# Window attention laid over eight shared PSUM banks, with new orders on all engines

## The reference, cut to what matters

```python
qkv = xw @ qkv_w + qkv_b                       # xw: (B * 16 windows, 64 tokens, 64 channels)
q, k, v = (split(t) for t in jnp.split(qkv, 3, axis=-1))          # 4 heads of 16
scores = jnp.einsum('bhqd,bhkd->bhqk', q, k)
scores = scores / jnp.maximum(qn * kn.transpose(0, 1, 3, 2), 1e-06) / jnp.clip(tau, 0.01)[None, :, None, None]
scores = scores + bias[None]                   # a table over relative positions, from a small MLP
scores = scores.reshape(B, NW, HEADS, TOK, TOK) + _MASK[None, :, None]
attn = jax.nn.softmax(scores.reshape(B * NW, HEADS, TOK, TOK), axis=-1)
out = jnp.einsum('bhqk,bhkd->bhqd', attn, v)   # then heads side by side
om = out @ proj_w + proj_b                     # windows back to image, rolled back
skip = xin + _layer_norm(om, ln1_g, ln1_b)
```

## Time and profile before

| what | us |
|---|---|
| median of 3 runs | 783.17 (781.18 to 783.38) |
| span of the profiled execution, first to last instruction | 778.6 |
| its own time beside the span | not listed; the median is 4.6 above the span |
| TensorE busy | 665.7 (86%) |
| VectorE busy | 516.4 (66%) |
| ScalarE busy | 480.4 (62%) |
| GpSimd busy | 355.1 (46%) |

### The profile page before, as it was taken

How to read it: one execution, slowest core, us unless ns; L and a number is a source line. 1 busy time by engine, 2 the same in 40 slices (tenths; PEclk the granted TensorE clock), 3 DMA queues, 4 the chain that set the end, 5 groups by cost and what they waited for, 6 DMA issues and landing times. The chain is left out here.

```text
span 778.6 us, 21192 instructions
## 1 busy us (share of the span) xinstructions
PE 665.7 (86%) x8584; PEld 371.4 (48%) x8584; DVE 516.4 (66%) x997; ACT 480.4 (62%) x963; POOL 355.1 (46%) x441
## 2 busy tenths in 40 slices
PE   4785789999999999999998579999999988749880
PEld 2562455565565555655555232233333367735350
DVE  4796487877777787877778322577777786372181
ACT  3565266777777777777775548877777656624000
POOL 4696446778777777788776520022221123100000
PEclk9787599999999999999999959999999999969955
DMA  9550000000000000000000020122112220120278
GB/s 216 137 128 11 1 3 2 3 2 3 2 3 3 3 3 3 3 2 3 3 2 3 2 56 1 28 55 56 33 50 55 55 55 2 31 72 2 63 194 269
DMA packets 15719, 31.44 MB, mean 40 GB/s; under 512 B 7488, under 2 KB 9284, under 8 KB 15620
## 3 DMA queue, kind: packets, MB, share of 16 engines
q1 hardware_dynamic: 12592, 29.16, 14.1%
q10 hardware_dynamic: 2760, 0.66, 0.5%
q0 software_dynamic: 272, 0.27, 0.2%
HBM read 20.71 MB, written 9.37 MB: 39 GB/s over the span
## 5 line engine op out<-in xcount | busy, mean ns | idle before, releaser
L794 POOL TENSOR_TENSOR sc<-sc,mx 128x512 f32<-128x512 f32 x128 | 133.7, 1044 | 102.4 <-DVE mx L725 102.4
L722 DVE TENSOR_TENSOR sc<-s_ps,bias_tab 128x512 f32<-128x512 f32 x128 | 87.7, 685 | 52.6 <-PE s_ps L528 52.6
L1424 POOL TENSOR_TENSOR square<-xs 128x1024 f32<-128x1024 f32 x16 | 34.1, 2133 | 165.5 <-DVE xs L1166 165.5
L539 PE MATMUL t_ps<-consts,sc 128*128 128x128 f32 x512 | 84.4, 288 | 16.2 <-ACT pt L656 12.5
L656 ACT ACTIVATE pt<-t_ps 128x512 f32<-128x512 f32 x128 | 75.7, 592 | 31.2 <-PE t_ps L539 30.1
L539 PEld LDWEIGHTS t_ps<-consts,sc 128*128 128x128 f32 x512 | 54.3, 142 | 84.8 <-issue 48.1
L725 DVE TENSOR_REDUCE mx<-sc 128x8 f32<-128x512 f32 x128 | 87.8, 686 | 4.4
L1081 ACT ACTIVATE hs<-h_ps,fb1s 128x512 f32<-128x512 f32 x128 | 78.2, 689 | 19.1 <-PE h_ps L990 19.0
L528 PE MATMUL s_ps<-kx,qu 32*64 32x128 f32 x2048 | 72.3, 278 | 3.5 <-DVE kx L749 2.9
L990 PE MATMUL h_ps<-xs,fw 64*128 64x512 f32 x256 | 68.7, 650 | 1.0 <-ACT hs L1081 1.0
L528 PEld LDWEIGHTS s_ps<-kx,qu 32*64 32x64 f32 x2048 | 56.7, 134 | 15.2 <-issue 13.4
(11 more groups left out here) (207 smaller groups left out, 1295.2 us busy)
## 6 DMA issues: line engine op xcount, KB each, us to landing
raw<-in_x_dram SPq DMA_DIRECT2D x32, 256.0 KB, 5.1
xr<-in_x_dram SPq DMA_DIRECT2D x32, 256.0 KB, 3.9
out_dram<-x SPq DMA_DIRECT2D x32, 256.0 KB, 3.9
rec_scratch<-r SPq DMA_DIRECT2D x4, 224.0 KB, 2.5
w<-in_L_conv_W_dram SPq DMA_DIRECT2D x1, 784.0 KB
w<-in_L_conv_W_dram SPq DMA_DIRECT2D x1, 672.0 KB
xs<-rec_scratch SPq DMA_DIRECT2D x16, 28.0 KB
xs<-rec_scratch ACTq DMA_DIRECT2D x16, 28.0 KB
```

The costliest lines, as they stand in the source:

```text
L539: last = pe.transpose(t_ps[:, m], sc[n % KEPT][:, m].rearrange("c h k -> c (h k)"), ident)
L722: dve.tensor_tensor(sc[n % KEPT][:, :, :, :], s_ps[j][:, :, :, :], bias_tab[:, j, hp], ALU.add)\
L794: pool.tensor_tensor(v, v, mx[n % KEPT][:, :].unsqueeze(2).broadcast_to([128, 8, TOK]), ALU.subtract)\
```

## The change

All eight banks become one tensor, `banks`, and each use names its bank; a bank passes from one use to the next by a semaphore. `score` runs twice a pair instead of four times: both halves `hp` of the head pairs at once, 32 matmuls on four row strips and two column halves, into four banks. Transposes have banks by turns instead of one; the sums are a group of their own (`sums`), apart from `mix`. `spread_rstd` has four matmuls of 32 rows into four banks, without the half-zero weights. Work on two 512-column halves becomes one instruction of 1024 columns on VectorE (bias, maximum, scaling) and ScalarE (copies; the spread of values in 4 instructions instead of 8). GpSimd keeps 512 columns each. `qu`, `kx`, `ob` exist once; score tiles, now double in size, three times. The four lists are new and run for 20 steps, and the special code for the last pair is gone.

```diff
-    def score(pe, p, q):
-            a, hp = q // 2, q % 2
-            pe.wait_ge(s["queries"], 2 * p + a + 1)
-            pe.wait_ge(s["keys_odd"], 2 * p + a + 1)
-            after(pe, s["biased"], 2 * (4 * p + q))
-            for i, m, w in WINDOWS:
-                for j in range(2):
-                    row = rows(2 * j + hp)
-                    last = pe.matmul(s_ps[j][TOK * w:TOK * (w + 1), 2 * i + m], qu[p % 2][a][row, at],
-                                     kx[p % 2][a][row, :, at], start=True, stop=True)
+    SCORE_BANKS = ((6, 2), (4, 6))
+    TURN_BANKS = {(0, 0): (2, 3), (0, 1): (5, 4), (1, 0): (5, 4), (1, 1): (0, 7)}
+    SUM_BANKS, MIX_BANKS = (5, 0), (6, 4)
+    def score(pe, p, a):
+            if a == 0:
+                pe.wait_ge(s["queries"], p + 1)
+                pe.wait_ge(s["keys_odd"], p + 1)
+                if there(p + 1, PAIRS):
+                    pe.wait_ge(s["q_out"], p + 2)
+            else:
+                pe.wait_ge(s["biased_00"], p + 1)
+                after(pe, s["heads_0"], p)
+                after(pe, s["exped_11"], 2 * p)
+                after(pe, s["normed"], 2 * (p - 2) + 2)
+            for i in range(2):
+                for m in range(2):
+                    for w in range(2):
+                        at = slice(TOK * (4 * i + 2 * m + w), TOK * (4 * i + 2 * m + w + 1))
+                        for j in range(2):
+                            for hp in range(2):
+                                row = rows(2 * j + hp)
+                                out_bank = banks[:, SCORE_BANKS[a][hp] + j].rearrange("c (m n) -> c m n", m=4)
+                                last = pe.matmul(out_bank[TOK * w:TOK * (w + 1), 2 * i + m], qu[row, a, at],
+                                                 kx[row, a, :, at], start=True, stop=True)
...
     def spread_rstd(pe, p):
-            for h in range(2):
-                for j, (lo, hi) in enumerate(HALVES):
-                    last = pe.matmul(spread_bank(p, j)[:, 256 * h:256 * (h + 1)], spread_half[lo:hi, h], rv[lo:hi, :],
+            for g in range(4):
+                last = pe.matmul(banks[:, 2 + g, 0:256], spread_image[rows(g)], rv[rows(g), :], start=True, stop=True)
...
+    def add_bias(dve, p, a, hp):
...
+            dve.tensor_tensor(sc[n % KEPT][:, :, :, :, :].rearrange("c j m h k -> c (j m h k)"),
+                              banks[:, first:first + 2].rearrange("c j n -> c (j n)"),
+                              bias_tab[:, hp].rearrange("c j m h k -> c (j m h k)"), ALU.add)\
+               .then_inc(s[f"biased_{a}{hp}"], 1)
+    def row_max(dve, p, a, hp):
...
+            dve.tensor_reduce(mx[n % KEPT][:, :], sc[n % KEPT][:, :, :, :, :].rearrange("c j m h k -> c (j m h) k"),
+                              X, ALU.max).then_inc(s[f"row_max_{a}{hp}"], 1)
...
     def tensor_step(pe, n):
+        project_keys(pe, n)
+        turn(pe, n - 2, 1, 0, 1)
+        score(pe, n - 1, 0)
+        sums(pe, n - 2, 0)
+        variances(pe, n - 3)
+        turn(pe, n - 2, 1, 1, 0)
+        turn(pe, n - 2, 1, 1, 1)
+        mix(pe, n - 2, 0)
+        spread_rstd(pe, n - 3)
+        norms(pe, n)
+        sums(pe, n - 2, 1)
+        score(pe, n - 1, 1)
+        turn(pe, n - 1, 0, 0, 0)
+        turn(pe, n - 1, 0, 0, 1)
+        values(pe, n - 1)
+        mix(pe, n - 2, 1)
+        spread_first(pe, n)
+        turn(pe, n - 1, 0, 1, 0)
+        turn(pe, n - 1, 0, 1, 1)
+        project_heads(pe, n - 2)
+        turn(pe, n - 1, 1, 0, 0)
+        project_queries(pe, n + 1)
     def vector_step(dve, n):
+        scale_keys(dve, n - 1, 1)
+        add_bias(dve, n - 1, 0, 0)
+        add_bias(dve, n - 1, 0, 1)
+        row_max(dve, n - 1, 0, 0)
+        divide(dve, n - 2, 0)
+        normalise(dve, n - 3, 0)
+        normalise(dve, n - 3, 1)
+        row_max(dve, n - 1, 0, 1)
+        add_bias(dve, n - 1, 1, 0)
+        add_bias(dve, n - 1, 1, 1)
+        row_max(dve, n - 1, 1, 0)
+        divide(dve, n - 2, 1)
+        row_max(dve, n - 1, 1, 1)
+        scale_queries(dve, n)
+        scale_keys(dve, n, 0)
     def scalar_step(act, n):
+        copy_queries(act, n)
+        exponent(act, n - 2, 1, 0, 0)
+        copy_keys(act, n)
+        exponent(act, n - 2, 1, 0, 1)
+        sum_log(act, n - 2, 0)
+        var_rstd(act, n - 3)
+        sum_exp(act, n - 2, 0)
+        exponent(act, n - 2, 1, 1, 0)
+        exponent(act, n - 2, 1, 1, 1)
+        norm_recip(act, n)
+        sum_log(act, n - 2, 1)
+        sum_exp(act, n - 2, 1)
+        by_rows(act, n - 3, 0, 0)
+        exponent(act, n - 1, 0, 0, 0)
+        exponent(act, n - 1, 0, 0, 1)
+        by_rows(act, n - 3, 0, 1)
+        by_rows(act, n - 3, 1, 0)
+        spread_values(act, n - 1)
+        by_rows(act, n - 3, 1, 1)
+        exponent(act, n - 1, 0, 1, 0)
+        exponent(act, n - 1, 0, 1, 1)
+        copy_projected(act, n - 2)
     def pool_step(pool, n):
+        square_projected(pool, n - 3, 0)
+        square_projected(pool, n - 3, 1)
+        square(pool, n, q_sb, q_sq, "q_out", "q_sq")
+        square(pool, n, k_sb, k_sq, "k_out", "k_sq")
+        shift(pool, n - 1, 0, 0)
+        skip(pool, n - 3, 0)
+        skip(pool, n - 3, 1)
+        shift(pool, n - 1, 0, 1)
+        shift(pool, n - 1, 1, 0)
+        shift(pool, n - 1, 1, 1)
```

More of the change, by code:

```diff
@@ L418, in build @@
                 "k_ps", "q_ps", "k_out", "q_out", "k_sq", "q_sq", "norm_ps", "norm_ln", "rnorm", "first_spread",
[L419 to L424, removed]
+                "keys_even", "keys_odd", "queries", "v_ps", "v_out", "heads_0", "heads_1", "proj_ps", "proj_out", "csq",
@@ L432, in build @@
[L432 to L445, removed]
@@ L512, in spread_first @@
+                    for a in range(2):
+                        last = pe.matmul(banks[:, 6 + a], spread_keys[rows(a)], rn[rows(a), :], start=True, stop=True)
                     last.then_inc(s["first_spread"], 1)
-                    for a in range(2):
-                        last = pe.matmul(b_ps[a][:, :], spread_all[rows(2 + a)], rn[rows(2 + a), :], start=True, stop=True)
-                    last.then_inc(s["first_spread"], 1)
-            def score(pe, p, q):
+            def score(pe, p, a):
@@ new lines, in sums @@
+            def sums(pe, p, a):
+                if there(p, PAIRS):
+                    pe.wait_ge(s[f"exped_{a}0"], 2 * p + 2)
+                    pe.wait_ge(s[f"exped_{a}1"], 2 * p + 2)
+                    if a == 0:
+                        pe.wait_ge(s["exped_10"], 2 * p + 1)
+                    for j in range(2):
+                        for hp in range(2):
+                            last = pe.matmul(banks[rows(2 * j + hp), SUM_BANKS[a]], ones, pt[a][2 * hp + j][:, :, :],
+                                             start=True, stop=True)
+                    last.then_inc(s[f"sum_ps_{a}"], 1)
@@ L542, in mix @@
             def mix(pe, p, a):
                 if there(p, PAIRS):
[L545 to L552, removed]
+                    pe.wait_ge(s["v_out"], p + 1)
@@ L581, in variances @@
                     pe.wait_ge(s["csq"], 2 * p + 2)
[L582 to L585, removed]
+                    if there(p + 3, PAIRS):
+                        pe.wait_ge(s["k_out"], p + 4)
                     for g in range(4):
                         half = slice(256 * (g % 2), 256 * (g % 2 + 1))
-                        last = pe.matmul(n_ps[rows(g), 0:256], mean_rows, csq[g // 2][:, half], start=True, stop=True)
+                        last = pe.matmul(banks[rows(g), 1, 0:256], mean_rows, csq[:, g // 2, half], start=True, stop=True)
                     last.then_inc(s["var_ps"], 1)
@@ L675, in by_rows @@
-            def by_rows(act, p, j):
+                    after(act, s["unrolled"], 2 * p)
+                    act.activation(cc[:, :, :], banks[:, 0:2], ACT.Identity, bias=bp[:, 0:1]).then_inc(s["proj_out"], 1)
+            def by_rows(act, p, j, i):
                 if there(p, PAIRS):
                     act.wait_ge(s["skipped"], 2 * p + j + 1)
-                    unroll(lambda dst, src: act.activation(dst, src, ACT.Copy), p, j).then_inc(s["unrolled"], 1)
-            def unroll(copy, p, j):
-                for i in range(2):
@@ L718, in bias_max @@
                 if there(p, PAIRS):
[L719 to L726 removed]
+                    n = 4 * p + 2 * a + hp
```

381 lines of the change are left out of this document (151 added, 230 removed).

## The result

The changed kernel takes 722.82 us (median of 4 runs, 720.4 to 723.61) against 782.17 (780.86 to 783.38) beside it: a ratio of 0.9236, 95% interval 0.921 to 0.9262. The profiled execution has a span of 721.5 instead of 778.6. The forecast was 731, in a range of 719 to 760.

What follows compares the result with a forecast made beforehand. TensorE (PE) was taken to bound the attention step: 21.25 - 2.06 - 0.50 - 0.30 = 18.4, plus 0.3 gives 18.7 us. With the stage's ends, 52 us earlier: 783.2 - 52 = 731 us, range 719 to 760.

Steps and rivals of the forecast that it cites:

- scores: PE's score matmuls: two groups of 1.03 us replace four of 1.03, saving 2.06 us a step.
- factor: PE's LayerNorm factor (spread_rstd): four row strips at once, 0.57 us instead of 1.07, saving 0.50 a step.
- changes of shape: PE's group order: a change of tile shape costs about 0.1 us; more same-shape neighbours save 0.30 a step.
- the stall of 0.78: PE's one gap per step, a transpose waiting for ScalarE to empty the only transpose bank; predicted to go.
- added for thin margins: 0.3 us added to PE's 18.4 a step, because PE arrives last at joins by only 0.25 to 0.6.
- step: One attention loop step, one pair of images: 22.03 us before, predicted 18.7, with 18.4 to 19.2 as range.
- the near row: Profile row used for score groups: doubled row strips, same number of rounds, so a group of 64 instructions takes 1.03 us.
- Ends: Attention stage's start and tail: second pair's keys at 83.8, last pieces 16.5 and 21, stage end at 401, 52 us earlier.
- The partial step: First step after the second pair's projection of keys, partly at the lower clock level: predicted 18 us.
- Rival 1: Attention loop: the ring of waits between engines sets the step, 20.2 us, giving 753 us; chance 0.20.
- Rival 2: PE scores: eight tiles run no faster than four, group 2.06, step 20.8, giving 763 us; chance 0.08.
- Rival 3: VectorE's long operations hold up GpSimd, whose operations take 1.5 us, 24 us a step, giving 816 us; chance 0.05.

Runs made afterwards that it cites:

- experiment 3: Changed kernel with the variances moved between two transposes, so two pairs of neighbours of one tile shape are lost: 724.03 us (0.9249).
- experiment 6: Changed kernel with unused VectorE maxima over 512 columns added each step before the scaling of queries and keys: one 723.65 us, three 743.32 us.
- experiment 2: Changed kernel with each score group cut in two halves and another group placed between them: 769.42 us (0.9855).
- experiment 5: Changed kernel with VectorE's bias and maxima back to two operations of 512 columns each: 723.22 us (0.9252).
- experiment 7: Changed kernel with the values on four 64x64 tiles: 714.08 us (0.9142); a variant on two strips of 64 rows by 128 columns: 724.06 us.

## Why the prediction was right

The mechanism was as forecast: PE's groups bound the step before and bind it after, and the experiments put PE time back and took it away with the step following by the same amount: 0.82 for 0.82, 0.42 for 0.41, and -0.69 for the values' -0.79 (the transposes ahead of them, no longer of one shape with them, cost 0.09 more). By its terms, in us a step:

| term | predicted | measured |
|---|---|---|
| scores | -2.06 (group of 1.03) | -1.84 (1.14) |
| factor | -0.50 (0.57) | -0.42 (0.65) |
| changes of shape | -0.30 | -0.73 |
| the stall of 0.78 | gone | gone |
| added for thin margins | +0.30 | 0 |
| step | 18.7 | 18.26 |

The errors partly cancel: scores and factor gave 0.30 less than forecast, changes of shape and margins 0.73 more. That the step came out within 0.44 is in part luck. No run gave the transposes their one bank back, so that the stall went because of the banks is argued and not shown.

- **Scores**: the near row held within 0.11. Eight row-and-column tiles do run at once: in the first half of a group the single records show rounds of eight instructions 109 ns apart, where before rounds of four were 109 ns apart. From 0.51 us on the instructions start one by one, some 17 ns apart, and the last starts 0.94 us after the first instead of 0.84: there the group's extra 0.11 lies. Why, no run shows. 1.14 us over 64 is 18 ns each; the floor of about 25 ns that the Trainium skill (TensorE: Matmul & The Clock Gate, Part 1) states, an estimated 1.6 us for the group, did not come.
- **Changes of shape** were mis-sized most: 0.1 for one, read from a transpose beside the values alone. Other pairs are worth more: 0.16 for two transposes (1.02 against 2 x 0.59), 0.16 for queries and keys (1.88 against 2 x 1.02), 0.12 for sums ahead of variances (0.88 against the 1.00 of experiment 3). The 0.73 is what is left of the step's 3.77 after the other terms. Summed from start to start over both steps, it lies in the transposes (0.50), queries and keys (0.16), sums (0.16), norms (0.11) and variances (0.02), less 0.22 for the mixes, which no longer stand beside their sums. Experiment 3 shows the price for two pairs; the rest is read from the timelines.
- **Margins**: the 0.25 to 0.6 us that I followed were about right (0.25, 0.56 and 0.64 measured), but a positive margin costs nothing. The 0.3 was caution and not a cost, and experiment 6 shows it for VectorE: one dose of 0.6 us costs 0.08, three (1.8 us) cost 1.27.
- **Other engines**: VectorE 15.42 (15.1 predicted), ScalarE 15.27 (15), GpSimd 16.65 (16.6).
- **Ends**: the second pair's keys start at 84.25 (83.8), though the stage itself begins 1.7 us later than before, since the stage ahead ended later in this execution. The partial step is 17.67 (18). The 14 steps come to 254.4 (one of 17.07, 13 of 18.26) instead of 262, and the rest to 38.9 instead of 37.5: 395.3 instead of 401.
- **The remaining 3 us** of the 8 by which 731 was too high are outside the stage. The prediction took 4.6, the median minus the profiled span, for the time around the span. It is 1.8: each run of either kernel here has its time 1.8 above its span (723.31 and 721.5, 782.79 and 781.0). So the profiled execution of the kernel before was itself 2.8 faster than the median, and the term was mis-read. The profiled execution of the changed kernel lay 0.5 above its median.

Rival 1 (the ring takes over) falls by experiment 6 and by PE's full stretch; it needs about 0.6 us more on VectorE. Its own sum, 15.5 + 4.3, is 19.8 and not the 20.2 that its time was worked out from. Rival 2 falls by the score group itself, 1.14 instead of 2.06; experiment 2 shows what it would have cost, 769 with the halves kept apart, near the 763 that it gave. Rival 3 falls by GpSimd's unchanged 1044 ns. Merging instructions on VectorE gains nothing by itself in the piece tested (experiment 5).

## What to carry to other kernels

Where a busy engine has no gap, count its groups from start to start and ask what each could cost with every tile of the array in use; what follows from that was good to 0.1 us a group. Order groups of one tile shape side by side, and look first at the width of the weights where a small matmul doesn't get faster. A margin in a ring of waits is free until it is used up, and a dose on one engine tells how large it is at that engine's joins.

## What the runs showed of the hardware

- Instructions on other row strips begin while those of the first strips still run, with no order written for it: 1.55 us for two halves in a row against 2.06 for two apart.
- 64 instructions on eight tiles of 32x64 take 1.14 us and 64 on four tiles of 64x64, with 64 moved columns, 1.09.
- A group ahead of one of another tile shape takes 0.09 to 0.16 us more on PE than ahead of one of its own (0.09 for the transposes ahead of the values in experiment 7, 0.16 for two transposes or for queries and keys).
- With 128 weight columns, moving 64 columns (1.93 us, rounds of 0.112) is no faster than moving 128 (1.88, 0.112).
- VectorE's and ScalarE's operations over two PSUM banks at once run as one: 1.22 us (L720) and 1.11 us (L690) for 1024 columns.
